# Differential attention with an FFN gate: one V projection a step later, and the combination and the low part earlier in a step

## The reference

```python
x  = L0_attn_hidden_states                 # (8, 512, 512)
xn = layernorm(x)
# attention: 16 query heads and 8 key heads of 128, in pairs; 4 value heads of 256
qkv = xn @ Wqkv_w.T + Wqkv_b
p1 = softmax(causal(q[..., 0, :] @ k[..., 0, :].T * D ** -0.5))
p2 = softmax(causal(q[..., 1, :] @ k[..., 1, :].T * D ** -0.5))
lam = exp(sum(lambda_q1 * lambda_k1)) - exp(sum(lambda_q2 * lambda_k2)) + LAMBDA_INIT
o = (p1 - lam * p2) @ v                    # v and k are shared by two query pairs
o = o * rsqrt(mean(o * o) + EPS) * subln_w * (1 - LAMBDA_INIT)
s = o.reshape(B, S, H * D) @ out_w.T + out_b
# gate: both operands rounded to 4-bit floats with one scale for 32 values
g = silu(mxfp4(xn) @ mxfp4(ffn_w).T + ffn_b)
out = x + s * g
```

## Time and profile before

| what | value |
|---|---|
| median of three runs | 1606.81 us |
| the profiled execution | 1607.1 us |
| its span, first to last instruction | 1605.3 us |
| mean granted TensorE clock | 0.983 |
| TensorE busy | 1486.7 us (93%) |
| TensorE weight loads | 864.8 us (54%) |
| VectorE busy | 1133.6 us (71%) |
| ScalarE busy | 876.8 us (55%) |
| POOL busy | 857.5 us (53%) |
| share of the chain that ended last | TensorE 52%, VectorE 16%, ScalarE 11%, POOL 9% |

### The profile page before, as it was taken

How to read it: one execution, slowest core, us unless ns; L and a number is a source line. 1 busy time by engine, 2 the same in 40 slices (tenths; PEclk the granted TensorE clock), 3 DMA queues, 4 the chain that set the end, 5 groups by cost and what they waited for, 6 DMA issues and landing times.

```text
span 1605.3 us, 27534 instructions
## 1 busy us (share of the span) xinstructions
PE 1486.7 (93%) x8982; PEld 864.8 (54%) x8982; DVE 1133.6 (71%) x2654; ACT 876.8 (55%) x2474; POOL 857.5 (53%) x1587
## 2 busy tenths in 40 slices
PE   5777879999999989999999999999999998999978
PEld 2444445556555556455565565556564555555644
DVE  5888877667775777757776677757777477775761
ACT  5666765366634666346653566336663466535650
POOL 2566546555465544655455554655546554554543
PEclk9989899999999999999999999999999999999989
DMA  8245453334423453235433335234441344333333
GB/s 262 62 87 132 89 91 65 91 81 74 88 56 89 84 87 76 48 95 84 91 64 91 81 64 96 65 86 83 91 79 43 96 85 90 63 70 76 65 65 73
DMA packets 382496, 134.76 MB, mean 84 GB/s; under 512 B 361872, under 2 KB 365968, under 8 KB 382352
## 3 DMA queue, kind: packets, MB, share of 16 engines
q1 hardware_dynamic: 382352, 132.99, 39.7%
HBM read 35.93 MB, written 8.39 MB: 28 GB/s over the span
## 4 chain that ended last, share of the span: by engine, by line
PE 52%; DVE 16%; ACT 11%; POOL 9%; issue 7%; DMA 4%; SPq 1%; ACTq 0%; POOLq 0%; DVEq 0%
PE ps L544 15%; PE ps L546 14%; PE ps L545 14%; ACT pp L713 4%; DVE ps L1011 3%; DVE qkv L976 3%; PE ps L611 3%; PE ps L613 3%; PE ps L612 3%; ACT ph L722 2%; DMA pT<-ph 2%; ACT qkv L690 2%; DVE ph L1023 2%; POOL qkv L1210 1%; ACT on L735 1%
## 5 line engine op out<-in xcount | busy, mean ns | idle before, releaser
L713 ACT ACTIVATE pp<-ps,row 128x384 f32<-128x384 f32 (+3 forms) x512 | 267.6, 523 | 262.9 <-DVE row L1011 262.7
L1226 POOL TENSOR_TENSOR row<-row,small 128x1 f32<-128x1 f32 x256 | 150.9, 590 | 431.5 <-ACT pp L713 431.5
L544 PE MATMUL ps<-xT,wqkv 128*128 128x512 f16 x768 | 295.6, 385 | 18.8 <-DVE qkv L976 7.8
L1011 DVE CUSTOM_DVE_ANT_0 ps<-ps,mask,ssc 128x384 f32<-128x384 f32 (+3 forms) x512 | 280.0, 552 | 37.5 <-PE ps L613 36.0
L545 PE MATMUL ps<-xT,wqkv 128*128 128x512 f16 x768 | 295.4, 385 | 0.0
L546 PE MATMUL ps<-xT,wqkv 128*128 128x512 f16 x768 | 295.4, 385 | 0.0
L1023 DVE SCALAR_TENSOR_TENSOR ph<-pp,small,ph 128x128 f16<-128x128 f32 (+3 forms) x256 | 152.7, 596 | 128.2 <-ACT ph L722 125.7
L544 PE MATMUL ps<-qkv,pT 128*128 128x256 f16 x640 | 177.6, 277 | 58.0 <-DMA pT<-ph 51.4
L722 ACT ACTIVATE ph<-pp,small 128x128 f16<-128x128 f32 (+3 forms) x256 | 141.4, 553 | 128.3 <-DVE pp L1017 126.5
L976 DVE SCALAR_TENSOR_TENSOR qkv<-ps,bsc,qkv 128x512 f16<-128x512 f32 x192 | 143.2, 748 | 94.0 <-ACT qkv L690 92.9
L544 PE MATMUL ps<-wout,heads 128*128 128x512 f16 x512 | 194.1, 379 | 2.4 <-DVE small L991 1.3
(11 more groups left out here) (132 smaller groups left out, 2977.2 us busy)
## 6 DMA issues: line engine op xcount, KB each, us to landing
xres<-in_x SPq DMA_DIRECT2D x32, 256.0 KB, 3.0
out_x<-res SPq DMA_DIRECT2D x32, 256.0 KB, 2.3
wqkv<-in_wqkv SPq DMA_DIRECT2D x15, 512.0 KB, 6.5
xin<-in_x SPq DMA_DIRECT2D x7, 1024.0 KB, 6.0
vbias<-in_bv SPq DMA_DIRECT2D x32, 128.0 KB, 3.3
pT<-ph SPq DMA_TRANSPOSE x256, 2.7
wout<-in_ow SPq DMA_DIRECT2D x8, 512.0 KB, 4.2
heads<-on SPq DMA_TRANSPOSE x128, 3.2
```

The lines of the kernel that those rows point to most:

```text
L544: mm(out, ah, bh, start=start and j == 0, stop=False)
L713: run(out, sc_ps[u][:, m, 0:w], ACT.Exp, bias=ebias[:, u, m:m + 1], scale=-1.0, accum_out=psum_l[:, n % 6, m:m + 1]).then_inc(exp_done, 1)
L1011: nc.vector.tensor_tensor_reduce(sc, sc, mask[:, S - w:S], ssc[:, c:c + 1], BIG, ALU.add, ALU.min, ebias[:, u, m:m + 1]).then_inc(max_done, 1)
```

## The change

Three edits. First, the list of steps for the eight projections of group 3 changes: the last Q, the first V and the last V projection each move one step later, to steps 20, 21 and 22 of the batch. Second, in steps without a late output VectorE does the combination ahead of the first maximum, and the low part of the probabilities between the two maxima. Third, ScalarE writes the high part of the probabilities ahead of the first exponential.

```diff
 # schedule(): steps, within the eight steps of the group, of k0 k1 q0 q1 q2 q3 v0 v1
-        at = (None, PROJ_AT, PROJ_AT, (0, 1, 1, 2, 3, 3, 4, 5))[g]
+        at = (None, PROJ_AT, PROJ_AT, (0, 1, 1, 2, 3, 4, 5, 6))[g]

 # ScalarE's loop
                 if n and not late:
                     square_o(n - 1)
+                if n + AHEAD - 1 < NSTEPS:
+                    p_hi(n + AHEAD - 1)
                 if n + AHEAD < NSTEPS and not late:
                     exps(n + AHEAD, 1)
-                if n + AHEAD - 1 < NSTEPS:
-                    p_hi(n + AHEAD - 1)

 # VectorE's loop
+                if n + AHEAD - 1 < NSTEPS:
+                    combine(n + AHEAD - 1)
                 if n + AHEAD < NSTEPS and not late:
                     maxima(n + AHEAD, 1)
                 if n + AHEAD - 1 < NSTEPS:
-                    combine(n + AHEAD - 1)
+                    p_lo(n + AHEAD - 1)
                 if n + AHEAD < NSTEPS and not late:
                     maxima(n + AHEAD, 0)
-                if n + AHEAD - 1 < NSTEPS:
-                    p_lo(n + AHEAD - 1)
```

## The result

The changed kernel took 1611.14 us, the median of eight runs (1609.7 to 1613.56), against 1605.68 for the kernel before (1601.55 to 1607.04). The ratio is 1.0039, 95% interval 1.0027 to 1.005: slower by 0.4%, where 0.2% faster was forecast. The profiled execution has a span of 1611.8 us, 6.5 more than before, at a mean granted clock of 0.982.

The account below looks back on a forecast made before the run. TensorE, busy for 93% of the span, was taken as the bound, so only its waits, mostly for pT, could be won. Terms -6.3 + 4.8 - 1.0 + 0 = -2.5 us took 1606.8 to 1604.3 us; own range 1599 to 1608, with rivals 1597 to 1611.

Parts of the forecast that it names:

- the gain, -6.3 us for steps 18 to 25: Batches 1 to 6: attention of step 23 comes 1.05 us sooner in each (bounds 0.6 and 1.5).
- The attention of step 23 ends the stall as before: Step 23: its wait for pT remains, so 1.05 us is the gain of steps 22 and 23 together.
- The waits of steps 24 and 25 stay: Steps 24 and 25, batches 1 to 6: TensorE's waits there were taken as unchanged.
- Up to the attention of step 22 TensorE has the same work as before: Steps 18 to 22: same TensorE work, but one 2.6 us fill moves from step 19 into step 22.
- the low part beside V's low half: Step 22: VectorE's low part meets POOL's V work for up to 0.4 us a batch; by the rule, sum 1606.7.
- The price in steps 8 to 15: Batches 1 to 6: the longer loop delays pT for step 15, 0.8 us a batch (0 to 1.4), +4.8 us.
- A: Rival: gain without the price, the lag of steps 10 to 14 being absorbed; 1598 us, chance 0.2.
- Steps 24 to 31: VectorE's waits for scores cover the combination and high part: no cost, or 0.3 us a batch without that cover.
- Batch 0: pT leads by up to 0.8 us, once and not per step: -1.0 us, between -4 and +4.
- The last batch: FFN fill of step 22 waits some 3 us, against gains in steps 24 to 26: 0, between -2.5 and +4.
- C: Rival: last batch, TensorE stands 3 us before step 22's FFN fill, then runs at 1.2 GHz; 1608 us, chance 0.1.
- B: Rival: slower, low part before second maximum lengthens the loop in every step with a projection; 1612 us, chance 0.2.

Follow-up runs that it names:

- e6: The whole change, but in step 22 VectorE reads the V fill ahead of the normalisation's low half; ratio 1.0012 to the kernel before.
- e1: Kernel before with only the new steps for group 3's projections, old order within a step; ratio 0.995.
- e5: Kernel before with the new placement, ScalarE as changed, and VectorE doing combination, both maxima, then low part; ratio 0.985.
- e2: Kernel before with the two reorderings on VectorE and ScalarE alone, old placement of the fills; ratio 1.0117.
- e7: The whole change, but with the new order in steps 16 to 23 of each batch alone; ratio 0.9978 to the kernel before.
- e3: Kernel before, old placement, ScalarE as changed, VectorE with combination first, both maxima, low part last; ratio 0.9938.
- e4: Kernel before, old placement, ScalarE as changed, VectorE with first maximum, combination, low part, second maximum; ratio 1.0442.
- e9: Kernel before, old placement and ScalarE's old order, VectorE with combination first, both maxima, low part last; ratio 1.0345.

## Why the prediction was wrong, step by step

**The step that failed is the gain, -6.3 us for steps 18 to 25 (1.05 us in each of six batches).** Measured: -2.2 us in steps 19 to 25 and +3.8 in steps 16 to 18, so +1.6 where -6.3 stood. Up to the attention of step 23 it went as written. The attention of step 22 is free, VectorE waits at the combination for POOL's coefficient (0.98 us), step 21 takes 5.00 us, and at the attention of step 23 the six batches are 5.0 us ahead (forecast 6.3; batch 2 alone has 1.8 of them, batch 1 none). "The attention of step 23 ends the stall as before" holds too, though the profile shows another wait in its place: e6 cut the bank's wait in batch 3 from 2.03 to 0.59 us, and the attention came 0.02 us sooner. That batch 1 has none of the lead goes with the lower clock there, which the prediction had priced for the last batch alone. Two sentences beside it were wrong.

First, "The waits of steps 24 and 25 stay". By the attention of step 24 only 2.1 of the 5.0 us are left: the FFN fill of step 24 now waits about 1 us for VectorE's gating in batches 3, 4 and 5, and that gating comes 27.95 us after TensorE's step 19 in batch 3, where it came after 28.17. VectorE itself is hardly ahead. It begins its step 23 behind a normalisation and a V read that end late: 22.1 to 22.3 us after TensorE's step 19 in the six batches, before 22.4, in e1 21.0 (20.8 in one batch). I had ended the account at the attention of step 23, and had not asked how far VectorE was ahead. The new order is not all of it. The step that follows (from the combination of step 23 to that of step 24, batch 3) takes 4.16 us and took 3.60, but it takes 4.16 in e5 and 3.99 in e1 too, and 3.54 in e2: its length goes with the placement. And e1 also gives back a part, 13.6 us ahead at step 23 and 9.0 at step 24. What the new order costs is already missing at the attention of step 23, 5.0 against 13.6.

Second, "Up to the attention of step 22 TensorE has the same work as before". The work is the same, but its fills wait: 0.15 to 0.22 us in step 17 (four batches) and 0.47 in step 18 (five) for VectorE's low half of a K or Q fill, and steps 16 to 18 are 3.8 us longer in all. The lag of step 15 was priced only at the `pT` of step 15, as if it ended there. e7 shows where it comes from: without the new order in steps 8 to 15 the stretch is +0.6.

A last point concerns the whole and not one term. e1 and e2 show that the placement alone gains 0.5% and the order alone loses 1.2%. I had the length of the new loop, 5.0 us for step 21 where the old order takes 3.80, and used it to find when step 22 starts, but compared the result with the kernel before and so booked a gain of the placement for the change as a whole.

On the low part beside V's low half, the Trainium skill ("SBUF — State Buffer", section "Who interferes with whom") lets a VectorE instruction with two SBUF inputs and a GpSimd instruction that reads SBUF exclude each other. The trace agrees that the low part gets longer, in step 22 of all six batches, but not by how much: it took 0.92 us and not 0.75, so 0.17 more, where it ran beside POOL's instruction for 0.37 (781.08 to 781.45). The case in the prediction is alike, 0.49 us more for 0.69 side by side (741.88 to 742.57), so "the trace agrees" said too much there. The measurement decides: the sum needed 0.17 a batch, not 0.4.

**The price in steps 8 to 15, +4.8, measured +7.1 and +5.9.** The mechanism held and the size was low, by less than single profiles scatter in this stretch (old order, e1 and e7: -2.1 and +2.5). The waits in steps 14 and 15 cost 10.4 us, and 4.7 come back in steps 11 and 12. That fits A's effect, `pT` sooner before the lag builds up, but it is not shown: e1, with the old order there, has -3.0 in the same two steps. The wait at step 15 is 0.8 to 0.9 us in five batches, as forecast in size, and 2.9 in batch 3. A second one, of 0.3 to 1.0 us at step 14, was not forecast. I counted the lag at step 15 alone, and held steps 10 to 12 to half of 0.56; the step lengths 4.19, 4.55 and 4.79 against 4.06, 4.18 and 4.51 give 0.13 + 0.37 + 0.28, and with the 0.54 of step 13 the lag is 1.32 (forecast 1.4). That sum was right. That the attention of step 14 had no slack either, I had not looked up.

**Steps 24 to 31, "at nothing"**: +1.1 us, nearly all in step 31, which is 0.1 to 0.6 us longer in each batch. The fallback of 0.3 a batch (1.8) was nearer.

**Batch 0**: -0.4 and -1.3 against -1.0, close. **The last batch**: -3.1 against 0, outside the bounds of -2.5 and +4. The gap before the FFN fill of step 22 came as forecast (3.1 us, forecast 3). In steps 22 to 25 together the clock was not lower than before but higher, 0.93 and before 0.82 (length, busy by engine, PEclk, DMA share, GB/s; before, then after):

```profile
1523.75:1548.44 24.69, 16.36 (x85) 8.83 (x82) 13.56 (x41) 10.74 (x36) 11.20 (x24) 0.82 0.29 56
...
1531.47:1554.76 23.29, 15.52 (x107) 10.06 (x107) 13.79 (x41) 12.26 (x39) 11.96 (x25) 0.93 0.29 57
```

(In steps 26 to 28 it was 0.86 and before 0.94; in the second profile 1.00.) So C's price was not paid. What gave the 3 us is not separated: the placement alone has -3.5 in this batch (e1), the order alone -1.3 (e2).

**Of the rivals** B was nearest: slower by the lengthened loop, at 1612. It is right in its mechanism (e2 1.0117, e3 0.9938: the low part between the maxima costs 1.8% of the time against the same kernel with it behind them) and in its place: the waits at steps 14 and 31 that the prediction named as B's sign came. And it has the better total by luck: it kept the gain of 6.3, set 4 us on batch 0 that were not lost, and did not see that the last batch would give 3 us. I gave it 0.2 because 5.18 us stood above TensorE's 4.87 in one kind of step only; e4 and e9 show how steep this is: with steps of 5.83 and 5.29 the run is 4.4% and 3.5% slower.

## What to carry to other kernels

When engines run a software pipeline in lockstep, write down for each order within the step both the length of its loop through all engines and how far into it the critical product is ready, and compare the first with what the bounding engine needs: a lead is won once, a longer loop is paid in every step. Carry such a lead or lag on until something absorbs it, for each engine by itself, and not to the first instruction that shows it. The longest new wait in a trace may cover another that ends at the same time: only taking it away tells what it is worth.

## What was not expected of the chip

VectorE's same 2654 instructions took 23.8 us more. The combination with 512 columns rose from 791 to 856 ns on average, with 256 columns from 530 to 597. One of POOL's small operations rose too, L1238 on 128x1 from 296 to 415 ns, while L1240 went from 600 to 573. After:

```profile
L1017 DVE SCALAR_TENSOR_TENSOR pp<-pp,row 128x512 f32<-128x512 f32 x64 | 54.8, 856 | 9.4 <-POOL row L1228 9.4
...
L1238 POOL TENSOR_TENSOR row<-row 128x1 f32<-128x1 f32 x256 | 106.2, 415 | 112.9 <-ACT ps L726 112.2 <-ACT heads L726 0.7
```

It goes with the combination's place at the head of a step: in e2, e3, e5 and e9, which have it there too, the mean is 856 or 857 ns, and in e4, with the first maximum ahead of it, 799. The six of the 64 that run beside nothing of POOL take 0.74 us, the other 58 take 0.87 on average. That both engines' operations get longer fits a shared access to SBUF; no run here took the one away to see the other.

Nor had I expected how much ScalarE's order is worth by itself: e9 and e3 differ in it alone, 1.0345 against 0.9938. And e5's ratio, 0.985, is below the product of e1 and e3, though their profiled spans say the reverse (14.7 and 13.7 us under the span before, and e5 24.6; e1's profiled execution was a fast one). Whether the two edits help each other stays open.
